# Shift rows of four tiles as one set of 24: one transpose into the relative scores' bank and one masked copy by VectorE

## The reference, cut to what matters

```python
idx = jnp.clip(r[None, :] - r[:, None], -M, M) + M          # M = 128
rpk = rel_k[idx]; rpv = rel_v[idx]
content = jnp.einsum('bhqd,bhkd->bhqk', q, k)
relative = jnp.einsum('bhqd,qkd->bhqk', q, rpk)
scores = (content + relative) / sqrt(16)
w = softmax(scores, axis=-1)
out = einsum('bhqk,bhkd->bhqd', w, v) + einsum('bhqk,qkd->bhqd', w, rpv)
```

## Time and profile before

| what | us |
|---|---|
| median of 3 runs | 2637.97 (2635.26 to 2641.08) |
| the profiled execution's own time | 2641.73 |
| span of the profiled execution | 2640.0 |
| PE busy | 2420.9 (92%) |
| DVE busy | 1828.1 (69%) |
| ACT busy | 1749.4 (66%) |
| POOL busy | 884.5 (34%) |
| L902 transposes in 600 to 2100 us | 376 of them, 4 in each of 94 sets |
| L1124 copies in 600 to 2100 us | 95, 584 ns each |

### The profile page before, as it was taken

How to read it: one execution, slowest core, us unless ns; L and a number is a source line. 1 busy time by engine, 2 the same in 40 slices (tenths; PEclk the granted TensorE clock), 3 DMA queues, 4 the chain that set the end, 5 groups by cost and what they waited for, 6 DMA issues and landing times. The chain is left out here.

```text
span 2640.0 us, 47807 instructions
## 1 busy us (share of the span) xinstructions
PE 2420.9 (92%) x15216; PEld 1184.1 (45%) x15216; DVE 1828.1 (69%) x4985; ACT 1749.4 (66%) x4026; POOL 884.5 (34%) x1977
## 2 busy tenths in 40 slices
PE   6838999999999999999999999999999999799998
PEld 3412444444444444444444444444444444567666
DVE  6558777777777777777777777777777774233333
ACT  4514877777777777777777777777777777321121
POOL 1222454333333333333333333333333332133332
PEclk9955999999999999999999999999999999999999
DMA  5668889777777777777777777777777762642221
GB/s 160 176 141 265 244 268 243 235 222 230 233 230 237 225 222 233 234 231 236 232 228 234 231 236 236 231 226 226 233 231 238 227 194 88 244 144 69 66 64 53
DMA packets 351151, 541.00 MB, mean 205 GB/s; under 512 B 30608, under 2 KB 259392, under 8 KB 350912
## 3 DMA queue, kind: packets, MB, share of 16 engines
q1 hardware_dynamic: 336880, 502.76, 61.8%
q0 software_dynamic: 14032, 35.24, 4.5%
HBM read 272.60 MB, written 269.43 MB: 205 GB/s over the span
## 5 line engine op out<-in xcount | busy, mean ns | idle before, releaser
L1073 DVE TENSOR_REDUCE part<-ps 128x1 f32<-128x512 f32 (+3 forms) x2048 | 1189.5, 591 | 457.8 <-PE ps L957 438.8
L1135 ACT ACTIVATE probs_T<-pst 128x512 f32<-128x512 f32 (+3 forms) x2048 | 985.3, 525 | 397.4 <-PE pst L966 390.0
L957 PE MATMUL ps<-k_front,q_front 96*128 96x512 bf16 x2048 | 790.1, 393 | 13.0 <-DVE part L1071 2.5
L915 PE MATMUL pout<-probs_T,v_far 128*32 128x512 f32 (+3 forms) x4864 | 550.8, 533 | 40.4 <-ACT probs_T L1111 31.4
L822 POOL TENSOR_TENSOR left_T<-probs_T,left_mask 128x128 f32<-128x128 f32 x512 | 219.5, 429 | 991.7 <-ACT probs_T L1111 797.4
L957 PEld LDWEIGHTS ps<-k_front,q_front 96*128 96x128 bf16 x2048 | 198.6, 97 | 587.8 <-DVE part L1073 296.8
L966 PE MATMUL pst<-q_back,k_left 102*128 102x512 bf16 (+3 forms) x1024 | 349.7, 343 | 0.7 <-ACT probs_T L1135 0.6
L966 PE MATMUL pst<-q_back,k_right 102*128 102x512 bf16 (+3 forms) x1024 | 348.8, 342 | 0.5
L1148 ACT ACTIVATE band<-band,negm 128x384 f32<-128x384 f32 (+1 forms) x512 | 305.5, 597 | 0.1
L1071 DVE CUSTOM_DVE_ANT_0 band<-ps,band 128x256 f32<-128x256 f32 (+2 forms) x704 | 300.5, 427 | 0.0
L915 PEld LDWEIGHTS pout<-probs_T,v_far 128*32 128x32 f32 x4864 | 174.5, 108 | 237.9 <-issue 211.4
(11 more groups left out here) (160 smaller groups left out, 2112.0 us busy)
## 6 DMA issues: line engine op xcount, KB each, us to landing
rel_scores<-rel SPq DMA_DIRECT2D x128, 1024.0 KB, 7.9
band_probs<-band SPq DMA_DIRECT2D x128, 768.0 KB, 3.9
pwin<-band_probs SPq DMA_DIRECT2D x128, 512.0 KB
band<-rel_scores SPq DMA_DIRECT2D x64, 768.0 KB
band<-rel_scores SPq DMA_DIRECT2D x64, 576.0 KB, 5.2
w<-in_w_dram SPq DMA_DIRECT2D x16, 1024.0 KB, 14.3
band<-rel_scores SPq DMA_DIRECT2D x64, 128.0 KB, 5.7
q_terms<-terms SPq DMA_DIRECT2D x48, 128.0 KB
```

The lines of the kernel that those rows point to most:

```text
L915: return nc.tensor.matmul(pout[32 * g:32 * g + 32, c0:c1], values, probs, start=first, stop=False, skip_group_check=True)
L957: nc.tensor.matmul(ps1[u % 2][:, :], q_front[a.par][:, a.s * P:(a.s + 1) * P], k_front[a.par][:, u * CW:(u + 1) * CW], start=True, stop=Tr ...
L1073: ins = nc.vector.tensor_reduce(peak, src, AX_X, ALU.max)
L1135: ins = nc.scalar.activation(probs_T[t.s % 2][:, u * CW + c0:u * CW + c1], pst[u % 2][:, c0:c1], ACT.Exp, scale=SCALE)
```

## The change

- SHIFTS is 24: the rows under `q_back` are now those of four tiles. `shb` is ordered (side, tile, term), and its 24 columns are transposed at once, into columns 320 to 383 of `prel` (128 bf16 values a row) in place of `psmall`.
- A copy by VectorE, at u = 2 of the same step behind the reduction of that quarter, writes all 24 rows x 512 columns: each row is repeated for the four tiles and multiplied by a mask (`own_tile`) that is 1 only in the tile that the row belongs to. `k_left` and `k_right` have 12 rows of ones and 12 of zeros. ACT's copy L1124 is gone.
- PE issues the transpose ahead of the relative scores L979 and no longer waits for `winT_evac` there. VectorE's copy waits for the transpose and for ACT's copy of the relative scores of this step (`r_evac`). L979 of the next step and `turn_back` wait for `rows_copied`; L1003 no longer does.
- GpSimd builds the mask once, with a memset, two affine selects and an add, ahead of the constants that the first steps wait for.

```diff
-SHIFTS = 6
+SHIFTS = 24
-        shb = two("shb", [P, CH, SHIFTS], BF16)
+        shb = two("shb", [P, 2, CH, 3], BF16)
+        own_tile = sb("own_tile", [SHIFTS, CH], BF16)
+        own_sides = sb("own_sides", [SHIFTS, 2, CH], BF16)
-        prow = psmall[0:SHIFTS, NEARW:512].bitcast(BF16)
+        ROW_AT = 320
+        prow = prel[0:SHIFTS, ROW_AT:ROW_AT + P // 2].bitcast(BF16)
...
                         wait(pe, rows_copied, y.count(4, y.r))
-                        if w.valid:
-                            wait(pe, winT_evac, w.count(16, w.s + 1))
-                        for g in range(CH):
-                            mm = nc.tensor.transpose(prow[0:SHIFTS, g * P:(g + 1) * P], shb[y.r % 2][:, g, :], con["ident_bf"][:, :])
-                        mm.then_inc(rows_tp, 1)
+                        if not x.valid:
+                            pe.wait_ge(r_evac, NBH * 16)
+                        nc.tensor.transpose(prow, shb[y.r % 2][:, :, :, :].rearrange("p k g t -> p (k g t)"), con["ident_bf"][:, :]).then_inc(rows_tp, 1)
...
                         wait(pe, norm_done, o.count(1, 0))
+                        pe.wait_ge(rows_copied, y.count(4, y.r + 1) if y.valid else NBH * 4)
                         wait(pe, r_evac, x.count(16, x.s + 1) if x.valid else NBH * 16)
...
+                            if off % CH == 2 and y.valid:
+                                shift_rows()
+                            if off % CH == 3 and y.valid:
+                                pe.wait_ge(rows_copied, y.count(4, y.r + 1))
                             nc.tensor.matmul(prel[:, 0:RELS], q_front[x.par][:, x.s * P:(x.s + 1) * P], con["rel_k"][:, :], start=True, stop=True).then_inc(r_mm, 1)
-                        if u == 1 and off % CH == 2 and y.valid:
+                        if u == 1 and off % CH == 2 and y.valid and not x.valid:
                             shift_rows()
...
-                        if off % CH == 2 and y.valid:
-                            pe.wait_ge(rows_copied, y.count(4, y.r + 1))
...
+                    def shift_rows():
+                        dve.wait_ge(rows_tp, q.count(4, q.r + 1))
+
+                        dve.wait_ge(r_evac, x.count(16, x.s + 1) if x.valid else NBH * 16)
+                        rows = q_back[q.par][ROWS:ALLROWS, q.r * CW:(q.r + 1) * CW].rearrange("p (g c) -> p g c", c=P)
+                        nc.vector.tensor_tensor(rows, prow.unsqueeze(1).to_broadcast([SHIFTS, CH, P]),
+                                                own_tile[:, :].unsqueeze(2).to_broadcast([SHIFTS, CH, P]), ALU.mult).then_inc(rows_copied, 1)
...
+                        if u == 2 and off % CH == 2 and q.valid:
+                            shift_rows()
...
-                    def shift_rows():
-
-                        act.wait_ge(rows_tp, shifted.count(4, shifted.r + 1))
-                        nc.scalar.activation(q_back[shifted.par][ROWS:ALLROWS, shifted.r * CW:(shifted.r + 1) * CW], prow, ACT.Copy).then_inc(rows_copied, 1)
```

More of the change, by code:

```diff
@@ L683, in near_columns @@
             return bl[0] * P, (bl[-1] + 1) * P
-        CONSTS = 18
+        CONSTS = 19
         with nc.Block() as block:
@@ L697, in step @@
                         sp.dma_start(rv_win[:, 1, 0:HD], io["rel_v"][M:2 * M, :]).then_inc(const_in, 16)
-                        sp.wait_ge(const_set, CONSTS + 3)
+                        sp.wait_ge(const_set, CONSTS + 6)
                     if off % NB == 0:
@@ L796, in _ @@
                 pool.memset(rv_left[:, :], 0.0).then_inc(const_set, 1)
+                pool.memset(own_sides[:, :, :], 1.0).then_inc(const_set, 1)
                 pool.memset(neg_scale[:, :], -SCALE).then_inc(const_set, 1)
@@ L802, in _ @@
                                    pattern=[[1, P]], channel_multiplier=-1).then_inc(const_set, 1)
+                pool.affine_select(out=own_sides[:, :, :], in_=own_sides[:, :, :], compare_op=ALU.is_ge, fill=0.0, base=0,
+                                   pattern=[[-3 * CH, 2], [-3, CH]], channel_multiplier=1).then_inc(const_set, 1)
+                pool.wait_ge(const_set, CONSTS + 2)
+                pool.affine_select(out=own_sides[:, :, :], in_=own_sides[:, :, :], compare_op=ALU.is_ge, fill=0.0, base=2,
+                                   pattern=[[3 * CH, 2], [3, CH]], channel_multiplier=-1).then_inc(const_set, 1)
+                pool.wait_ge(const_set, CONSTS + 3)
+                nc.gpsimd.tensor_tensor(own_tile[:, :], own_sides[:, 0, :], own_sides[:, 1, :], ALU.add).then_inc(const_set, 1)
                 pool.wait_ge(const_in, 16 * 4)
@@ L805, in _ @@
                 nc.gpsimd.tensor_tensor(rv_win[:, :, 0:HD], rv_win[:, :, 0:HD], rv_ends[:, :, :], ALU.subtract).then_inc(const_set, 1)
-                pool.wait_ge(const_set, CONSTS + 3)
+                pool.wait_ge(const_set, CONSTS + 6)
                 zero_sides = zero[:, :, :].unsqueeze(3).to_broadcast([P, CH, 2, M - 1])
@@ L828, in step @@
                         four = slice(4 * y.r, 4 * y.r + 4)
-                        t = shb[y.r % 2][:, :, :].rearrange("p g (k t) -> p g k t", k=2)
+                        t = shb[y.r % 2][:, :, :, :].rearrange("p k g t -> p g k t")
                         pool.wait_ge(rmax_ready, g + 1)
@@ L946, in step @@
                             pe.wait_ge(shift_set, 8)
-                            pe.wait_ge(const_set, CONSTS + 3)
+                            pe.wait_ge(const_set, CONSTS + 6)
                         pe.wait_ge(back_in[t.par], t.count2(144, 144))
@@ L1014, in _ @@
                 for p in range(2):
-                    nc.vector.memset(k_left[p][ROWS:ROWS + 3, :], 1.0).then_inc(shift_set, 1)
-                    nc.vector.memset(k_right[p][ROWS:ROWS + 3, :], 0.0).then_inc(shift_set, 1)
-                dve.wait_ge(const_set, CONSTS + 3)
+                    nc.vector.memset(k_left[p][ROWS:ROWS + 3 * CH, :], 1.0).then_inc(shift_set, 1)
+                    nc.vector.memset(k_right[p][ROWS:ROWS + 3 * CH, :], 0.0).then_inc(shift_set, 1)
+                dve.wait_ge(const_set, CONSTS + 6)
                 def step(hb, off):
@@ L1023, in step @@
                     last = Step(hb, off - 1)
+                    q = Step(hb, off - 6)
+                    x = Step(hb, off + LAG_R)
                     four = slice(4 * last.r, 4 * last.r + 4)
@@ L1098, in step @@
                     y = Step(hb, off - 5)
-                    shifted = Step(hb, off - 6)
                     w = Step(hb, off - LAG_T - 1)
@@ L1140, in step @@
                             relative()
-                        if u == 1 and off % CH == 2 and shifted.valid:
-                            shift_rows()
                     if y.valid:
```

## The result

| | before | after |
|---|---|---|
| median us (4 runs each) | 2639.32 (2635.26 to 2641.08) | 2700.23 (2689.84 to 2700.96) |
| span of the profiled execution | 2640.0 | 2698.4 |
| one head | 63.40 | 65.18 |
| PE / DVE / ACT busy | 2420.9 / 1828.1 / 1749.4 | 2433.3 / 1919.3 / 1682.1 |

The changed kernel is slower: ratio 1.0225, 95% interval 1.0208 to 1.0241. The forecast was 2666 in a range of 2650 to 2683. The sign was right, but the loss was forecast at 28 us and measured at 61.

A forecast was written before the change was run, and what follows sets the result against it. PE, 92% busy, was taken as the bound. 31 x (-0.49 + 0.16 + 0.26) + 30 x 0.92 = +25.4 us, with +2 at the start, gave +27.5 and 2666 us; range 2650 to 2683.

The forecast's parts named there:

- What could be won at u = 1: In PE's wait before the value sum: 0.56, 0.50, 0.44 and 0.43 us won at positions 2, 6, 10 and 14.
- What VectorE's copy costs: VectorE's new 512-element copy after the third quarter's reduction: 0.69 us of the engine, bounds 0.60 and 0.78.
- Position 6: Step with `turn_back`, which waits for the copy because it writes the shift rows' bank: +0.92 us, 30 times.
- rival 1: At VectorE's copy: writing from partition 96, it overlaps neither neighbour and takes 0.78 us; +40, 2678 us; chance 0.30.
- Position 2: Step where VectorE has room, but `pst` at u = 3 needs this set: -0.49 us, 31 times.
- Positions 10 and 14: Steps where VectorE's copy delays its fourth reduction and PE's next `ps`: +0.16 and +0.26 us, 31 times each.
- Start, GpSimd's mask, 120 rows: First head of `attend`: +2 us from three copies; GpSimd's mask built in idle time and 120 contraction rows: nothing.
- Rival 2: At VectorE's copy: it streams two bf16 values at a time, taking 0.33 us; -6, 2632 us; chance 0.08.
- Rival 3: Behind position 6: `turn_back`'s wait is given back through fewer waits for ACT's near copy; +2, 2640 us; chance 0.07.

## Why the prediction was right and wrong

- **What could be won at u = 1: half right.** The waits for the window copy went. At positions 6 and 10, where the near copy decides, the gain was 0.50 and 0.39 for the 0.50 and 0.44 forecast. At 2 and 14 I charged 0.06 for the transpose, half of what four of them had taken in the earlier trace rows. That row was of transposes among themselves with `pout` behind; in its new place the price was 0.25. This step failed: 0.19 of the gain was missing in each of the two steps, and the run that moves the transpose gets 0.53 in a head back, 16 us.
- **What VectorE's copy costs: mis-sized.** Its duration was right (684 ns for 0.69). I took 0.69 of the engine between bounds of 0.60 and 0.78; it was 0.84, outside both. The upper bound added two overlaps of 0.09 but not the 0.03 to 0.04 that the engine lets pass behind each end. The choice was the worse mistake: rival 1 named the mechanism and the place, and the Trainium skill, "VectorE: DVE Perf Modes", section "Two Vector instructions with no wait between them", gave its rule; I kept it at 0.30 because no row showed two such neighbours. With that rule the trace agrees: held at output partition 96, not held at 0, where the reductions write. The section names no price; the runs show 0.12 on either side, 0.75 in a head and 23 us in all.
- **Position 6: right in kind, the largest term.** The wait was forecast at 1.4 us, some 43 us in all, and was 44.4 us in 29 waits. The step lost 1.13 for 0.92: the copy 0.12 later, and `turn_back` 0.26 behind its end (1051.74 to 1052.00) where I took 0.15.
- **Position 2: too good.** -0.21 for -0.49. Half of the missing 0.28 is lost by u = 3, where PE was 0.42 ahead and not 0.56; the other half is the `pst` at u = 3 that needs this set: it waits 0.22, where I had 0.07.
- **Positions 10 and 14:** +0.30 and +0.56 for +0.16 and +0.26, from the same two terms, the held copy and the transpose.
- **Start, GpSimd's mask, 120 rows:** the first head took 0.5 more for the 2 forecast, but it differs by up to 4 us among the kernels here, so it tells little. The first scores came 0.9 later, within their spread of 7. The 120 rows cost nothing visible: `pst` still shows 0.38.
- **The rivals.** Rival 1's mechanism held, but its price of 0.78 was too low as well. Its 2678 and the 16 us of the transpose's place make 2694; the rest is the larger price of the copy and what lies outside the heads. Rival 2 fell: 684 ns is the duration of the other 512-element operations. Rival 3 fell: positions 7 to 9 are unchanged, and the run that removes the wait at position 6 keeps the whole of it.
- **The range** took rival 1 in as its far end and held no unpriced PE term beyond 0.06; with no bounds of its own on the transpose, and 0.78 as the most for a copy that took 0.84, it could not reach the result.

## What to carry to other kernels

Before a small instruction goes between two of a full in-order engine, look at the partition its output starts at and at how full the engine is there. The change made the kernel 2.3% slower with its copy behind the third reduction, at partition 96, and 2.1% faster with the copy a quarter earlier, out of a bank that nobody needs soon, at partition 0. Price an edit by the repeated part of the trace: here the start alone moved by 7 us from kernel to kernel, enough to hide one effect and to enlarge others. A buffer that is borrowed brings every later writer of its bank as a new waiter: list them with the time each is due before choosing the bank. And give every moved instruction bounds of its own, the cheap ones too.

## What the runs showed of the hardware

- A VectorE instruction whose output starts at partition 96 among neighbours that write from partition 0 started 0.72 us after a 0.69 us reduction, and the next one 0.72 after it; at partition 0 both gaps were 0.60. With 4 elements a row it took 0.17 us and added 0.32 to the engine's list.
- One transpose of 128 columns cost PE 0.25 us ahead of a matmul of 257 columns and nothing measurable behind it. With two semaphore waits taken from it and put ahead of an earlier matmul the 0.25 stayed, and three of four steps grew by 0.09 at the new place.
